# Seven blocks of 128 query columns for the maxima, and new orders on TensorE

## The chip, the core and the metric

The kernel runs on one core of a Trainium2 chip. The time is the device time of one execution in microseconds. Three runs of the kernel before took 1652.04 to 1652.82 us, median 1652.7.

## The reference, cut to what matters

A cross-attention layer and a routed feed-forward layer, both with a residual. Only the attention is touched.

```python
# x: (16, 224, 512); context: (16, 750, 384); 16 heads of 32
q = layernorm(x) @ Wq.T + bq
k = context @ Wk.T + bk
v = context @ Wv.T + bv
attn = softmax(einsum('bihd,bjhd->bhij', q, k) / sqrt(32))
x = x + einsum('bhij,bjhd->bihd', attn, v) @ Wo.T + bo
```

The softmax of each query and head runs over 750 keys.

## The kernel before, in words

The attention is cut into 64 groups: 16 batches of four groups, each with four heads (NG = 4, GH = 4). Python unrolls the loop over g, and each engine runs its own written list of steps, `first`, `second`, `third` or `fourth` by the group's position in its batch (g % 4). Semaphores alone tie the engines together. The expert layer follows after the last group.

While TensorE works on the scores of group g, it also prepares group g + 1 (maxima) and g + 2 (projections). Its steps are these; the short names are used in the tables below.

- Q: `project_q(g + 2)`, 12 matmuls of 224 columns. K0, K1: `project_k(g + 2, 0 or 1)`, 9 matmuls each.
- X0 to X7: `score_for_max(g + 1, u)` (L1529). A block of query columns of one head (QP = 112 of the 224) is the stationary operand, the keys in two halves of 376 columns are the moving one. The queries lie in `q_own`, a copy for each head with the other heads' rows set to zero. There is one pair of PSUM banks, X, so each block waits until DVE has taken the maximum of the block before (`max_done`).
- mT: `transpose_max(g + 1)` turns the column maxima round. ACT negates them into `mneg` (`max_out`, L765), behind the group's last exponential in its list, and SP sends them by DMA (`put_max`, L391) into a row of `qst`, so that the score matmuls subtract the maximum. Score 0 of the next group waits for that DMA.
- S0 to S11: `score(g, s)`, two matmuls of 224 columns into one of two PSUM banks S; ACT takes the exponential (`exps`, L773), so S(s) waits for the exponential s - 2.
- W0, W1, W2: `values(g, p)`, fp32 matmuls of the exponentials with V, after exponentials 4p to 4p + 3; W2 of a group runs in the next group's list.
- den: `denominators(g - 1)`, fp32 matmuls over `psum_p`, the sum of the exponentials that POOL builds in five additions of two tiles (`add_step`).
- In single positions: V4a to V5b and V0a to V3b, `project_v` in two parts; Oa, Ob and Oc, Od, `project_o` for the two halves of the rows; xT0, xT1, yT0, yT1, transposes; lg0, lg1, `logits`.

DVE's list is the same in all positions up to small additions: maximum 0, q_lo, maximum 1, maximum 2, k_lo 0, maximum 3, k_lo 1, (in the second position two `xT_rest`), invert and normalise of the denominators, maximum 4, `o_lo` (L1089), maxima 5, 6, 7, with `residual`, `keep_logits`, `y_stats` or `ln_stats` beside or behind the last ones. `o_lo` computes the low part of the output from `o_s` and `oT_h`, both in SBUF.

The blocks Q, K, V, O, den, transposes, logits and mT share three PSUM banks M in the fixed order of `misc_units` (L90): each takes the bank that was used three units earlier, and waits until it is freed. In the second position den takes the bank of K1, which DVE's k_lo 1 (L1057) frees.

In the first position POOL adds the output bias to `x_res` (`add_bo`, L498) at the end of its list, when SP's load of `x_res` (L358) has landed; that load waits for the stores of `x_res` (L368), which SP issues behind the copies of q and k into `qst` and `kst`. POOL's additions 3 and 4 of the group follow in the next position's list.

Of the kernel before, what the change touches and what calls it, by code (L numbers as in the profile page):

```python
# [6 lines left out]
F32R = mybir.dt.float32r  # L7
# [4 lines left out]
P = 128  # L12
# [8 lines left out]
GH = 4  # L21
# [46 lines left out]
XU = 8  # L68
# [50 lines left out]
def expert_phase(nc, x1_d, w1, b1, w2, b2, centroids, w_route, ident_d, gates_dram, out):  # L119
    x, ctxT, wqT, bq, wkT, bk, wvT, bv, woT, bo, ident, x1 = SCRATCH["attention"]  # L120
    with ExitStack() as es:
# [50 lines left out]
        mneg = sb("mneg", [XU, QP], F32R)  # L172
# [159 lines left out]
        with nc.Block() as block:  # L332
# [352 lines left out]
            def _(act):  # L685
# [335 lines left out]
            def _(dve):  # L1021
# [44 lines left out]
                def maximum(g, u):  # L1066
# [5 lines left out]
                    dve.tensor_reduce(mx[0:QP, u:u + 1], X[0:QP, :, 0:HALF[0][1]], AX.XY, ALU.max).then_inc(max_done, 1)  # L1072
# [99 lines left out]
                def first(g, b):  # L1172
# [13 lines left out]
                    maximum(g + 1, 7)  # L1186
# [3 lines left out]
                def second(g, b):  # L1190
# [16 lines left out]
                    maximum(g + 1, 7)  # L1207
                    residual(b - 1, 1)

                def third(g, b):  # L1210
# [13 lines left out]
                    maximum(g + 1, 7)  # L1224
                    y_stats(b - 1)

                def fourth(g, b):
# [13 lines left out]
                    maximum(g + 1, 7)  # L1241
# [197 lines left out]
            def _(pe):  # L1439
# [89 lines left out]
                def score_for_max(g, u):  # L1529
                    if not 0 <= g < GROUPS:  # L1530
                        return
                    j, qt = u // QT, u % QT
                    if u == 0:
                        pe.wait_ge(kh_done, 2 * (g + 1))
                    if qt == 0:
                        pe.wait_ge(own_done, GH * g + j + 1)
                    if g or u:
                        pe.wait_ge(max_done, XU * g + u)
                    for i, (off, w) in enumerate(HALF):
                        last = pe.matmul(X[0:QP, i, 0:w], q_own[:, g % 2, j, QP * qt:QP * (qt + 1)],  # L1540
                                         kh_s[:, g % 2, off:off + w], start=True, stop=True)
                    last.then_inc(x_full, 1)

                def transpose_max(g):
# [4 lines left out]
                    pe.transpose(out[0:XU, 0:QP], mx[0:QP, :], id_s[0:QP, 0:QP]).then_inc(full, 1)  # L1549
# [79 lines left out]
                def first(g, b):  # L1629
# [4 lines left out]
                    values(g - 1, 2)  # L1634
                    score(g, 0)
                    score(g, 1)
                    score_for_max(g + 1, 2)
                    project_k(g + 2, 1)
                    score_for_max(g + 1, 3)
                    score(g, 2)  # L1640
                    denominators(g - 1)
                    project_v(b, 4, 0)
                    score_for_max(g + 1, 4)
                    score(g, 3)
                    score(g, 4)
                    project_v(b, 4, 1)
                    project_v(b, 5, 0)
                    score(g, 5)
                    project_v(b, 5, 1)
                    score_for_max(g + 1, 5)  # L1650
                    score(g, 6)
                    score(g, 7)
                    values(g, 0)
                    score(g, 8)
                    score_for_max(g + 1, 6)
                    values(g, 1)
                    score(g, 9)
                    score_for_max(g + 1, 7)
                    logits(b - 2, 0)
                    logits(b - 2, 1)  # L1660
                    score(g, 10)
                    score(g, 11)
                    transpose_max(g + 1)

                def second(g, b):
                    score_for_max(g + 1, 0)
                    project_q(g + 2)
                    score_for_max(g + 1, 1)
                    project_k(g + 2, 0)
                    values(g - 1, 2)  # L1670
                    score(g, 0)
                    score_for_max(g + 1, 2)
                    score(g, 1)
                    score(g, 2)
                    project_k(g + 2, 1)
                    score_for_max(g + 1, 3)
                    score(g, 3)
                    score(g, 4)
                    transpose_x(b + 1, 0)
                    transpose_x(b + 1, 1)  # L1680
                    values(g, 0)
                    denominators(g - 1)
                    score(g, 5)
                    project_o(b - 1, 0, 0)
                    score_for_max(g + 1, 4)
                    project_o(b - 1, 0, 1)
                    score(g, 6)
                    score(g, 7)
                    score_for_max(g + 1, 5)
                    score(g, 8)  # L1690
                    values(g, 1)
                    score_for_max(g + 1, 6)
                    project_o(b - 1, 1, 0)
                    score(g, 9)
                    score_for_max(g + 1, 7)
                    project_o(b - 1, 1, 1)
                    score(g, 10)
                    score(g, 11)
                    transpose_max(g + 1)

                def third(g, b):
                    project_q(g + 2)
                    score_for_max(g + 1, 0)
                    project_k(g + 2, 0)
                    score_for_max(g + 1, 1)
# [5 lines left out]
                    score(g, 2)  # L1711
                    score_for_max(g + 1, 3)
                    project_v(b + 1, 0, 0)
                    project_v(b + 1, 0, 1)
# [179 lines left out]
```

## Time and profile before

| what | value |
|---|---|
| median of three runs | 1652.7 us |
| profiled execution, its time | 1648.43 us |
| its span | 1646.6 us |
| TensorE busy | 1524.2 us, 93% |
| DVE busy | 1030.6 us, 63% |
| ACT busy | 944.2 us, 57% |
| POOL busy | 1080.2 us, 66% |
| maxima on DVE (L1072) | 512, 480.6 us busy |
| matmuls of score_for_max (L1540) | 1024, 272.0 us busy |

Busy times are of the whole span, with the expert layer, whose work starts some 1330 us in. Matmuls overlap their neighbours in these records, so a share of busy time is not a share of peak.

### The profile page before, as it was taken

How to read it: one execution, taken by the hardware profiler on the slowest of the kernel's cores; microseconds unless marked ns; L12 is line 12 of the kernel's file. 1: busy time of each engine (PE TensorE's matmuls, PEld its weight loads, DVE VectorE, ACT ScalarE, POOL GpSimd, SP SyncE). 2: the span in 40 equal slices, each digit the busy share in tenths (PEclk: the TensorE clock that was granted, in tenths of full speed). 3: DMA queues.
4: the chain of work that ended last, by engine and by line, in shares of the span. 5: the costliest groups of instructions: out<-in, count | busy, mean ns of one | idle time of the engine just before them, and what ended most of it. 6: DMA issues, size and time to landing. Idle time of an engine off the chain costs nothing.

```text
span 1646.6 us, 33344 instructions
## 1 busy us (share of the span) xinstructions
PE 1524.2 (93%) x11534; PEld 1247.4 (76%) x11534; DVE 1030.6 (63%) x1475; ACT 944.2 (57%) x2055; POOL 1080.2 (66%) x931
## 2 busy tenths in 40 slices
PE   4899999999999999999999999999999743899997
PEld 4777777778787878787877877877777433798996
DVE  5556666666666676766666666666665568344443
ACT  4456666666666666666666666665665440455554
POOL 3366767676767677776676777777775740477675
PEclk9999999999999999999999999999999765899999
DMA  7556666666667676767666757676756733578785
GB/s 193 97 81 111 101 134 123 110 124 108 127 110 134 111 129 112 131 110 139 112 130 107 136 101 144 101 140 101 140 91 120 187 122 35 136 135 147 135 148 90
DMA packets 113394, 199.29 MB, mean 121 GB/s; under 512 B 20448, under 2 KB 49280, under 8 KB 113104
## 3 DMA queue, kind: packets, MB, share of 16 engines
q1 hardware_dynamic: 98992, 165.81, 54.4%
q0 software_dynamic: 14240, 31.35, 10.5%
q8 instruction: 98, 1.61, 0.5%
q14 instruction: 64, 0.52, 0.1%
HBM read 64.29 MB, written 38.66 MB: 63 GB/s over the span
## 4 chain that ended last, share of the span: by engine, by line
PE 86%; DVE 5%; ACT 3%; POOL 2%; issue 1%; DMA 1%; POOLq 0%; DVEq 0%; SPq 0%; ACTq 0%
PE M L320 12%; PE S L1563 12%; PE M L321 12%; PE M L322 12%; PE X L1540 11%; PE O L1579 10%; ACT pr L781 2%; PE M L1825 2%; PE X L1807 2%; PE X L1808 2%; PE X L1806 2%; PE M L1826 2%; PE M L1827 2%; PE M L1590 2%; PE S L1796 2%
## 5 line engine op out<-in xcount | busy, mean ns | idle before, releaser
L1072 DVE TENSOR_REDUCE mx<-X 112x1 f32<-112x752 f32 x512 | 480.6, 939 | 356.0 <-PE X L1540 353.9
L491 POOL TENSOR_TENSOR psum_p<-psum_p,pr 125x896 f32<-125x896 f32 x256 | 543.9, 2124 | 172.6 <-ACT pr L781 149.1
L781 ACT ACTIVATE pr<-S 125x448 f32<-125x448 f32 x768 | 395.0, 544 | 224.4 <-PE S L1563 216.6
L1563 PEld LDWEIGHTS S<-qst,kst 128*125 128x125 f32 x1536 | 234.7, 189 | 113.0 <-ACT pr L781 51.2
L1563 PE MATMUL S<-qst,kst 128*125 128x224 f32 x1536 | 287.3, 291 | 27.1 <-ACT pr L781 21.2
L1540 PE MATMUL X<-kh_s,q_own 128*112 128x376 f32 x1024 | 272.0, 347 | 8.4 <-DVE mx L1072 7.9
L1540 PEld LDWEIGHTS X<-kh_s,q_own 128*112 128x112 f32 x1024 | 153.9, 176 | 48.0 <-issue 26.8
L1579 PE MATMUL O<-pr,v 125*32 125x224 f32 x3072 | 188.6, 364 | 1.7 <-ACT pr L781 1.7
L488 POOL TENSOR_TENSOR psum_p<-pr 125x896 f32<-125x896 f32 x64 | 135.6, 2119 | 80.1 <-ACT pr L781 79.9
L475 POOL TENSOR_TENSOR ctx_l<-ctx_r,ctx_h 128x750 fp32r<-128x750 f32 x48 | 85.4, 1811 | 74.7 <-ACT ctx_h L696 74.7
L320 PE MATMUL M<-ctx_h,wk_h 128*128 128x376 f32 (+1 forms) x384 | 130.0, 339 | 0.0
L321 PE MATMUL M<-ctx_l,wk_h 128*128 128x376 f32 (+1 forms) x384 | 129.4, 337 | 0.0
L322 PE MATMUL M<-ctx_h,wk_l 128*128 128x376 f32 (+1 forms) x384 | 128.8, 335 | 0.0
L1579 PEld LDWEIGHTS O<-pr,v 125*32 125x32 f32 x3072 | 81.3, 110 | 62.3 <-issue 23.1
L662 POOL DMA_INDIRECT out<-y_out,table_t x63 | 99.9, 1586 | 41.4 <-ACT y_out L1003 23.3
L654 POOL DMA_INDIRECT xg<-rows_d,table_x x63 | 62.4, 990 | 86.3 <-DVE settled L1400 43.0
L320 PE MATMUL M<-wv_h,ctx_h 128*125 128x512 f32 x288 | 116.8, 405 | 0.0
L322 PE MATMUL M<-wv_h,ctx_l 128*125 128x512 f32 x288 | 113.6, 394 | 0.0
L321 PE MATMUL M<-wv_l,ctx_h 128*125 128x512 f32 x288 | 113.5, 394 | 0.0
L1079 DVE RECIPROCAL M<-M 128x224 f32<-128x224 f32 x64 | 99.8, 1559 | 21.7 <-PE M L1590 21.6
L738 ACT ACTIVATE q_own<-qh_s,own 128x224 fp32r<-128x224 f32 x256 | 102.6, 472 | 2.1
L1062 DVE SCALAR_TENSOR_TENSOR kl_s<-M,bk_s,kh_s 128x376 fp32r<-128x376 f32 (+1 forms) x128 | 77.0, 602 | 14.3 <-ACT kh_s L749 14.1
(222 smaller groups left out, 3005.1 us busy)
## 6 DMA issues: line engine op xcount, KB each, us to landing
kst<-kh_s SPq DMA_DIRECT2D x128, 375.0 KB, 7.3
kst<-kl_s SPq DMA_DIRECT2D x64, 375.0 KB, 10.4
ctx_r<-ctxT SPq DMA_DIRECT2D x48, 375.0 KB, 12.2
qst<-qh_s SPq DMA_DIRECT2D x128, 112.0 KB, 2.8
rows_d<-x_res SPq DMA_DIRECT2D x32, 448.0 KB, 10.6
w_l<-w SPq DMA_DIRECT2D x16, 512.0 KB, 7.0
x_ln<-x SPq DMA_DIRECT2D x17, 448.0 KB, 11.0
qst<-ql_s SPq DMA_DIRECT2D x64, 112.0 KB, 3.0
```

The lines of the kernel that those rows point to most:

```text
L320: pe.matmul(out, lhs[0], rhs[0], start=first, stop=False)
L321: pe.matmul(out, lhs[0], rhs[1], start=False, stop=False)
L322: return pe.matmul(out, lhs[1], rhs[0], start=False, stop=last)
L488: pool.tensor_tensor(out=total, in0=tiles[0], in1=tiles[1], op=ALU.add).then_inc(sum_step, 1)
L491: pool.tensor_tensor(out=total, in0=total, in1=tiles[half], op=ALU.add).then_inc(sum_step, 1)
L662: pool.indirect_dma_start(out=out[:, :], out_offset=bass.IndirectOffsetOnAxis(ap=table_t[:, i:i + 1], axis=0), in_=y_out[:, i % YO, :], in ...
L738: act.activation(q_own[:, g % 2, j, :], qh_s[:, g % 2, :], ACT.Copy, scale=own[:, j:j + 1]).then_inc(own_done, 1)
L781: act.activation(pr[0:KP, (3 * g + p) % 2, j, :, :], S[0:KP, n % SB, 0:2 * NQ].rearrange("p (i n) -> p i n", i=2), ACT.Exp).then_inc(exp_d ...
L1072: dve.tensor_reduce(mx[0:QP, u:u + 1], X[0:QP, :, 0:HALF[0][1]], AX.XY, ALU.max).then_inc(max_done, 1)
L1540: last = pe.matmul(X[0:QP, i, 0:w], q_own[:, g % 2, j, QP * qt:QP * (qt + 1)], kh_s[:, g % 2, off:off + w], start=True, stop=True)
L1563: last = pe.matmul(S[0:KP, n % SB, NQ * h:NQ * (h + 1)], kst[:, i, j, o:o + KP], qst[:, i, j, :], start=True, stop=True)
L1579: last = pe.matmul(O[HD * j:HD * (j + 1), 0:NQ], v[0:KP, 2 * p + i, HD * j:HD * (j + 1)], pr[0:KP, (3 * g + p) % 2, j, i, :], start=(p == ...
```

## The change

The 4 x 224 = 896 query columns of the four heads are taken as one row of columns and cut into seven blocks of 128 in place of eight of 112. XU becomes 7, a block waits for the last head that it reaches into, and the maximum and the transpose use all 128 partitions. `mneg` becomes 7 x 128. DVE's lists lose maximum 7. TensorE's four lists are written anew. The lists of ACT and of POOL, and SP's, stay as they are.

```diff
-XU = 8
+XU = GH * NQ // P
...
-        mneg = sb("mneg", [XU, QP], F32R)
+        mneg = sb("mneg", [XU, P], F32R)
...
-                    act.activation(mneg[:, :], bank_of("mT", g)[0:XU, 0:QP], ACT.Copy, scale=-1.0).then_inc(freed("mT", g), 1)
+                    act.activation(mneg[:, :], bank_of("mT", g)[0:XU, 0:P], ACT.Copy, scale=-1.0).then_inc(freed("mT", g), 1)
...
-                    dve.tensor_reduce(mx[0:QP, u:u + 1], X[0:QP, :, 0:HALF[0][1]], AX.XY, ALU.max).then_inc(max_done, 1)
+                    dve.tensor_reduce(mx[:, u:u + 1], X[:, :, 0:HALF[0][1]], AX.XY, ALU.max).then_inc(max_done, 1)
...
                     maximum(g + 1, 6)
-                    maximum(g + 1, 7)
...
-                    j, qt = u // QT, u % QT
+                    own_q = q_own[:, g % 2, :, :].rearrange("p j n -> p (j n)")
                     if u == 0:
                         pe.wait_ge(kh_done, 2 * (g + 1))
-                    if qt == 0:
-                        pe.wait_ge(own_done, GH * g + j + 1)
+                    pe.wait_ge(own_done, GH * g + (P * (u + 1) - 1) // NQ + 1)
                     if g or u:
                         pe.wait_ge(max_done, XU * g + u)
                     for i, (off, w) in enumerate(HALF):
-                        last = pe.matmul(X[0:QP, i, 0:w], q_own[:, g % 2, j, QP * qt:QP * (qt + 1)],
+                        last = pe.matmul(X[:, i, 0:w], own_q[:, P * u:P * (u + 1)],
                                          kh_s[:, g % 2, off:off + w], start=True, stop=True)
...
-                    pe.transpose(out[0:XU, 0:QP], mx[0:QP, :], id_s[0:QP, 0:QP]).then_inc(full, 1)
+                    pe.transpose(out[0:XU, 0:P], mx[:, :], id_s[:, :]).then_inc(full, 1)
```

TensorE's lists in the short names, before and after:

```
first   before  X0 Q K0 X1 W2 S0 S1 X2 K1 X3 S2 den V4a X4 S3 S4 V4b V5a S5 V5b X5 S6 S7 W0 S8 X6 W1 S9 X7 lg0 lg1 S10 S11 mT
        after   X0 Q K0 X1 S0 W2 S1 X2 K1 S2 den X3 S3 V4a V4b S4 X4 S5 V5a V5b S6 X5 S7 lg0 W0 lg1 S8 X6 S9 W1 S10 mT S11
second  before  X0 Q X1 K0 W2 S0 X2 S1 S2 K1 X3 S3 S4 xT0 xT1 W0 den S5 Oa X4 Ob S6 S7 X5 S8 W1 X6 Oc S9 X7 Od S10 S11 mT
        after   X0 Q X1 W2 K0 S0 S1 X2 S2 K1 X3 S3 xT0 xT1 den X4 S4 S5 Oa Ob S6 S7 W0 X5 Oc S8 W1 S9 S10 X6 Od S11 mT
third   before  Q X0 K0 X1 S0 W2 S1 X2 K1 S2 X3 V0a V0b S3 den X4 V1a S4 S5 V1b X5 W0 S6 X6 S7 S8 S9 X7 W1 S10 mT S11
        after   Q W2 X0 K0 X1 K1 S0 X2 S1 V0a X3 S2 V0b S3 S4 den W0 S5 X4 V1a V1b S6 X5 S7 S8 X6 S9 W1 S10 S11 mT
fourth  before  X0 Q W2 X1 K0 X2 S0 S1 K1 S2 X3 den V2a S3 V2b X4 S4 S5 V3a V3b X5 S6 S7 W0 X6 W1 S8 S9 yT0 yT1 X7 S10 mT S11
        after   X0 Q K0 X1 W2 S0 S1 X2 K1 S2 X3 den S3 V2a V2b V3a S4 S5 V3b S6 S7 W0 X4 W1 X5 yT0 yT1 S8 X6 S9 S10 mT S11
```

## Rows read from the trace of the kernel before

**Rows 1.** Windows, 400 to 600 us: busy us and count of each engine, clock, DMA
```profile
400.00:600.00 200.00, 197.02 (x1537) 158.49 (x1534) 133.81 (x188) 123.31 (x278) 142.53 (x128) 1.00 0.66 116
```

**Rows 2.** Timeline of TensorE, one batch: start, duration, instruction, idle before
```profile
607.47 0.26 PE L1549 MATMUL M<-id_s,mx 112*8 112x112 f32 x1
...
684.95 0.58 PE L1540 MATMUL X<-kh_s,q_own 128*112 128x376 f32 x2
686.36 0.47 PE L1563 MATMUL S<-qst,kst 128*125 128x224 f32 x2 [0.83 <-ACT pr L781]
686.67 0.26 PE L1549 MATMUL M<-id_s,mx 112*8 112x112 f32 x1
```

**Rows 3.** Timeline of TensorE in a fourth position: starts of neighbouring blocks
```profile
671.68 0.51 PE L1540 MATMUL X<-kh_s,q_own 128*112 128x376 f32 x2
672.02 0.60 PE L1563 MATMUL S<-qst,kst 128*125 128x224 f32 x4
...
674.22 0.50 PE L1540 MATMUL X<-kh_s,q_own 128*112 128x376 f32 x2
674.65 0.58 PE L1590 MATMUL M<-psum_p,ones 125*32 125x224 f32 x8
```

**Rows 4.** The page's groups: busy us, mean ns, idle before; weight loads of score_for_max
```profile
L1540 PEld LDWEIGHTS X<-kh_s,q_own 128*112 128x112 f32 x1024 | 153.9, 176 | 48.0 <-issue 26.8
```

**Rows 5.** Waits of TensorE: us in total, times, longest
```profile
PE S L1563 <- ACT pr L781: 21.2, 36, 2.3
...
PE X L1540 <- DVE mx L1072: 7.9, 10, 1.7
```

**Rows 6.** Groups by line and shape: K's weight loads, POOL's bias additions
```profile
L320 PEld LDWEIGHTS M<-ctx_h,wk_h 128*128 128x128 f32 x384 | 73.7, 192 | 0.0
...
L507 POOL TENSOR_TENSOR x_res<-x_res,bo_s 112x512 f32<-112x512 f32 x30 | 38.1, 1290 | 28.2 <-DMA x_res<-x 28.2
```

**Rows 7.** Timeline of DVE, tail of a fourth position
```profile
678.99 2.33 DVE L1093 SCALAR_TENSOR_TENSOR oT_l<-o_s,bv_s,oT_h 128x224 fp32r<-128x224 f32 x1
...
682.93 0.94 DVE L1072 TENSOR_REDUCE mx<-X 112x1 f32<-112x752 f32 x1 [0.75 <-PE X L1540]
```

**Rows 8.** Timeline of SyncE's queue, end of a fourth position
```profile
608.81 0.71 SPq L393 DMA_DIRECT2D qst<-mneg  x1
```

**Rows 9.** Chain of waits, near the last group
```profile
1282.88 1.79 DMA qst<-mneg
```

**Rows 10.** Timeline of all engines, a second position (it begins at 627.4)
```profile
629.80 2.54 POOL L507 TENSOR_TENSOR x_res<-x_res,bo_s 112x512 f32<-112x512 f32 x2 [2.33 <-DMA x_res<-x]
...
632.30 4.38 POOL L491 TENSOR_TENSOR psum_p<-psum_p,pr 125x896 f32<-125x896 f32 x2
...
635.12 0.51 PE L1540 MATMUL X<-kh_s,q_own 128*112 128x376 f32 x2
...
636.52 0.60 DVE L1062 SCALAR_TENSOR_TENSOR kl_s<-M,bk_s,kh_s 128x374 fp32r<-128x374 f32 x1
...
637.55 0.56 PE L1590 MATMUL M<-psum_p,ones 125*32 125x224 f32 x8
...
641.17 0.44 DVE L1093 SCALAR_TENSOR_TENSOR oT_l<-o_s,bv_s,oT_h 128x224 fp32r<-128x224 f32 x1
```

**Rows 11.** Timeline of ACT, a fourth position: V3 copied out, exponentials 6 and 7
```profile
680.66 0.39 ACT L761 ACTIVATE v<-M 125x256 f32<-125x256 f32 x1 [0.98 <-PE M L322]
...
681.23 0.98 ACT L781 ACTIVATE pr<-S 125x448 f32<-125x448 f32 x2
```

**Rows 12.** Timeline of POOL, the same position: its additions
```profile
678.96 2.12 POOL L488 TENSOR_TENSOR psum_p<-pr 125x896 f32<-125x896 f32 x1
682.28 4.34 POOL L491 TENSOR_TENSOR psum_p<-psum_p,pr 125x896 f32<-125x896 f32 x2 [1.20 <-ACT pr L781]
```

**Rows 13.** Timeline of DVE after the last maxima: subtractions of the expert weights
```profile
1301.28 1.23 DVE L1149 TENSOR_TENSOR w_l<-w_l,w_h 128x1024 fp32r<-128x1024 f32 x1 [0.91 <-ACT w_h L846]
1303.57 4.99 DVE L1149 TENSOR_TENSOR w_l<-w_l,w_h 128x1024 fp32r<-128x1024 f32 x2 [1.07 <-ACT w_h L846]
```

More of the change, by code:

```diff
@@ L1633, in first @@
                     score_for_max(g + 1, 1)
[L1634 to L1705, printed above, removed]
                     score(g, 0)
@@ L1733, in third, with second @@
                     score(g, 11)
+                def second(g, b):
+                    score_for_max(g + 1, 0)
+                    project_q(g + 2)
+                    score_for_max(g + 1, 1)
+                    values(g - 1, 2)
+                    project_k(g + 2, 0)
+                    score(g, 0)
+                    score(g, 1)
+                    score_for_max(g + 1, 2)
+                    score(g, 2)
+                    project_k(g + 2, 1)
+                    score_for_max(g + 1, 3)
+                    score(g, 3)
+                    transpose_x(b + 1, 0)
+                    transpose_x(b + 1, 1)
+                    denominators(g - 1)
+                    score_for_max(g + 1, 4)
+                    score(g, 4)
+                    score(g, 5)
+                    project_o(b - 1, 0, 0)
+                    project_o(b - 1, 0, 1)
+                    score(g, 6)
+                    score(g, 7)
+                    values(g, 0)
+                    score_for_max(g + 1, 5)
+                    project_o(b - 1, 1, 0)
+                    score(g, 8)
+                    values(g, 1)
+                    score(g, 9)
+                    score(g, 10)
+                    score_for_max(g + 1, 6)
+                    project_o(b - 1, 1, 1)
+                    score(g, 11)
+                    transpose_max(g + 1)
@@ new lines, in third @@
+                def third(g, b):
+                    project_q(g + 2)
+                    values(g - 1, 2)
+                    score_for_max(g + 1, 0)
+                    project_k(g + 2, 0)
+                    score_for_max(g + 1, 1)
+                    project_k(g + 2, 1)
+                    score(g, 0)
+                    score_for_max(g + 1, 2)
+                    score(g, 1)
+                    project_v(b + 1, 0, 0)
+                    score_for_max(g + 1, 3)
+                    score(g, 2)
+                    project_v(b + 1, 0, 1)
+                    score(g, 3)
+                    score(g, 4)
+                    denominators(g - 1)
+                    values(g, 0)
+                    score(g, 5)
+                    score_for_max(g + 1, 4)
+                    project_v(b + 1, 1, 0)
+                    project_v(b + 1, 1, 1)
+                    score(g, 6)
+                    score_for_max(g + 1, 5)
+                    score(g, 7)
+                    score(g, 8)
+                    score_for_max(g + 1, 6)
+                    score(g, 9)
+                    values(g, 1)
+                    score(g, 10)
+                    score(g, 11)
+                    transpose_max(g + 1)
```

45 lines of the change are left out of this document (21 added, 24 removed).

## The prediction, made before the changed kernel ran

> **What bounds the kernel now.** I read the mean work of each engine in a steady stretch first, then the page's groups for the touched line, then who waited for whom on TensorE, and last the timelines of each engine over one batch of four groups. In the stretch TensorE is busy 197.02 of 200 us with the clock granted in full, DVE 133.81, ACT 123.31, POOL 142.53 [rows 1]. TensorE is what a group's length follows; the other three set only where it stalls. A group is about 20 us, a batch 686.67 - 607.47 = 79.20 us [rows 2].
>
> A pipelined matmul's busy time overlaps its neighbour's, so I price blocks by start to next start. One score_for_max takes 672.02 - 671.68 = 0.34 us [rows 3], though its two matmuls show 0.51 busy there. In front of a block of values or denominators (fp32 operands) the same block takes 674.65 - 674.22 = 0.43 [rows 3]: TensorE pays 0.09 for the change of operand kind. It is paid on entering values and denominators and on leaving any fp32 block, transposes and logits among them.
>
> Over that batch the blocks and changes leave 2.75 us of real waits: none in the first position, 0.77 in the second, 0.76 in the third, 1.2 in the fourth. The idle column shows only part of a wait, since a modelled tail covers the start of it: the largest, 684.95 + 0.34 to 686.36, is 1.07 us, of which the row shows 0.83 [rows 2]. The others are read in the same way, each as the time by which a block outlasts its price. All waits for exponentials show 21.2 us of idle time, all waits of a score_for_max for the maxima 7.9 [rows 5].
>
> **What the change does, term by term.** The summary speaks of four engines; the diff reorders only TensorE. ACT and POOL keep their lists, DVE loses the eighth maximum. So new places on TensorE meet old places elsewhere.
>
> (a) One score_for_max less in each group: 4 x 0.34 = -1.38 us a batch. The blocks that stay stream the same two times 376 columns. Their stationary operand widens from 112 to 128 columns: its load goes from 176 ns [rows 4] to the 192 ns that K's loads take [rows 6]. I take nothing for it, because X and K blocks keep the same 0.17 us per 376 columns with either width; with the loads exposed it would be 16 ns x 14 x 4 = +0.9 a batch. On DVE a maximum still reads 752 elements of each partition: 0.94 us [rows 7], one fewer, hidden. The copy out becomes 7x128 instead of 8x112 and its DMA carries the same 3.5 KB: nothing. Transposing needs one wait fewer.
> The Trainium skill speaks against this point: TensorE: Matmul & The Clock Gate, Part 2, says that the time of a weight load grows with its columns. The loads of rows 4 and 6 agree (176 to 192 ns); the page also says that the next load runs beside the current matmul, and by that the sum stays, while by the first sentence alone the +0.9 would be due.
>
> (b) Changes of operand kind, counted by the rule above: 10, 7, 9 and 10 in the four positions before, 8, 9, 7 and 10 after (values now stand between the logits in the first; denominators adjoin values in the third but no longer in the second). Two fewer: 2 x 0.09 = -0.19.
>
> (c) The waits. I lay each new list out by the block times and look at each semaphore.
>
> First position: maxima come at least 1.65 us apart (0.60 from the start of the block to DVE, 0.94, about 0.1 back); everything fits, also score 0, which moves ahead of values(g - 1, 2) by 1.0 us and needs the negated maxima. Their DMA is issued 608.81 - 607.47 = 1.34 after the transpose [rows 2, 8] and took 1.79 where the chain of waits ran through it [rows 9]: 3.1, against 3.9 in the new list. If it needed a microsecond more, that would cost 0.2 a batch. Waits 0, as before.
>
> Second: denominators moves ahead of values(g, 0) and so 1.3 us nearer to two things. It takes the PSUM bank of K1, which DVE frees after maximum 3 and k_lo: 2.0 us after that score_for_max starts (635.12 to 637.12) [rows 10]. In the new list only a score and two transposes (1.4 with the block itself) lie between: a wait of 0.6. And it needs POOL's last sum, which ended 636.68 before (two additions of 2.19 behind two bias additions that waited 2.33 for the x_res load) [rows 10], 9.3 us into a group that began 627.4; that wait is 28.2 / 14 = 2.0 on average [rows 6], so POOL ends 9.0 in. The load is issued by SP behind a store that starts in the first position, so a first position shorter by 0.4 puts it 0.4 later: 9.4. TensorE comes 8.8 in. Together 0.75 (bounds: 0.6, the bank alone, and 1.4, should the load be 0.8 late). Score 2 waits 0.17 for the first exponential. Sum 0.92.
>
> Third: score_for_max 3 now comes 1.25 us after number 2: waits 0.39. project_v(b + 1, 1) ends right before score 6; ACT copies its two halves first and reaches exponential 6 0.57 us after it starts on them (680.66, 681.23) [rows 11], and one exponential is 0.54: score 8 waits 0.58. score_for_max 6 waits 0.23. Sum 1.20.
>
> Fourth: its tail is the worst place. In the kernel before, maximum 4 is long done when o_lo runs. o_lo is the one steady operation of DVE with both inputs in SBUF; it starts 678.99 and takes 2.33 us, ending 0.24 after POOL's addition of 678.96 to 681.08 [rows 7, 12]; in the other three positions it takes 0.44 [rows 10]. Now score_for_max 4 stands behind values(g, 0), so maximum 4 ends 1.2 us after exponential 7, when POOL is in its second addition (it began 682.28, 0.07 after exponential 7 ended [rows 11, 12]). o_lo stands behind maximum 4 and in front of 5. It gets through when the addition ends, 2.45 after exponential 7; maximum 5 ends 3.35, score_for_max 6 starts 3.4, its maximum ends 4.95, the transpose starts 5.05. Before, it started 686.67 - 682.21 = 4.46 [rows 2, 11]. Exponential 7 itself comes 0.3 earlier. In waits: 0.2 for score_for_max 5, 0.7 for 6, 0.9 at the transpose: 1.80. The old wait of 1.07 on exponential 8 goes, but what is late next is the maximum of block 6. If o_lo were not held, the transpose would come 0.75 sooner.
>
> New waits 0 + 0.92 + 1.20 + 1.80 = 3.92, old 2.75: +1.17.
>
> **The sum.** -1.38 - 0.19 + 1.17 = -0.40 us a batch. The full pattern runs for 62 groups, 15.5 batches: -6.2 us. At the start, where three maxima in a row set the pace, one is saved in a place where there are still three: -0.35, inside the rounding. After the last group nothing changes. The profiled execution took 1648.43 us (span 1646.6): 1642.2. The runs shown have their median 4.3 above the profiled one: 1652.7 - 6.2 = 1646.5 us.
>
> **Rivals.**
> 1. The waits stay as they were, and all of 1.38 + 0.19 comes through: 15.5 x 1.57 = 24 us, 1628. For it: TensorE is busy nearly throughout, and idle shown is small [rows 1, 5]; it needs the order to dodge the banks and the second addition, which the rows above speak against. A nearer form, in which only o_lo in the fourth position isn't held, gives -0.40 - 0.75 = -1.15 a batch, -18, 1635. Chance of the two together 0.22.
> 2. Slower: o_lo is passed over by POOL. Its second and third additions follow each other (4.34 us for two [rows 12]). If the third got in before o_lo, o_lo would end 4.6 after exponential 7, and all behind it 2.2 later: 15.5 x 2.2 = +34 on the forecast, 1680. Against it: where both engines press, DVE's two-input subtractions and POOL's additions alternate: two in 4.99 us after one alone in 1.23 [rows 13]. It need not be the whole addition: from 0.4 us a batch the gain is gone, from 0.6 the kernel is slower by what can be told, and if it happens in two batches of five it is 0.9 on average, 1660, which I take as this rival's value. Chance 0.17.
> The Trainium skill, SBUF — State Buffer, Terms, calls the pair of ports that DVE and GpSimd share exclusive, held for the full instruction. By it o_lo waits for one addition as rows 7 and 12 show; it doesn't say who is next, which is what this rival turns on.
> 3. No change: denominators in the second position waits 1.1 in place of 0.75, as it does when the x_res load lands 0.5 later than on average: -0.05 a batch, 1652. Chance 0.18.
> 4. The change does not do what it says, since three engines keep their order: true of the text of it, and already in the sum.
>
> **How the numbers follow.** Forecast 0.43 (1640 to 1649), rivals as above. What a measurement here can tell from no change is 0.2%, 3.3 us. Faster by more: the forecast's 0.43 less a little at its upper edge, and rival 1: 0.61. Within: 0.2. Slower: 0.19. The range for 8 in 10 reaches down over rival 1's nearer half and most of its farther, 1629, and up over rival 3 and the first part of 2, to 1656.
>
> **What the changed profile would show.** 896 matmuls of score_for_max at 0.17 us start to start, so the width is free. TensorE's waits for the maxima up from 7.9 to over 15 us, at the transpose above all in the fourth position; waits of denominators for POOL or DVE in the second position in most batches, where there were none; o_lo still 2 us or so once a batch, but now between maxima 4 and 5 and shorter (it meets an addition already running). A batch of 78.8 us. I am wrong if a batch is under 78.2 or above 79.2: then one of the three lists of waits is wrong, and the position whose length differs says which.

## The result, and the profile after

The changed kernel took 1659.15 us (median of 5 runs, 1657.51 to 1660.19), the one before 1652.04 (1651.11 to 1652.82). The ratio is 1.0043, interval 1.0028 to 1.0057: slower by 7.1 us, where 6.2 us faster was forecast. The profiled execution took 1657.51 us, its span is 1655.6.

The page after, the groups that answer to [rows 4, 5] (busy us, mean ns, idle before):

```profile
PE 1505.5 (91%) x11406; PEld 1234.8 (75%) x11406; DVE 950.7 (57%) x1411; ACT 944.1 (57%) x2055; POOL 1079.9 (65%) x931
...
L1072 DVE TENSOR_REDUCE mx<-X 128x1 f32<-128x752 f32 x448 | 420.2, 938 | 461.4 <-PE X L1535 461.1
...
L1535 PE MATMUL X<-kh_s,q_own 128*128 128x376 f32 x896 | 246.7, 357 | 21.6 <-DVE mx L1072 21.1
L1535 PEld LDWEIGHTS X<-kh_s,q_own 128*128 128x128 f32 x896 | 139.3, 191 | 69.3 <-issue 67.2
```

The work that was to go is gone: 448 maxima in place of 512, 896 matmuls in place of 1024, TensorE's busy time down by 18.7 us. The span is 9 us longer. In windows over the stretch of [rows 1] (columns as there), TensorE is busy 3.7 us less at the same full clock, and DVE 15.4 less:

```profile
400.00:600.00 200.00, 193.33 (x1522) 155.79 (x1521) 118.42 (x175) 123.39 (x277) 141.18 (x127) 1.00 0.65 115
```

The waits of TensorE (us in total, times, longest) say what fills it. Those of score_for_max for a maximum went from 7.9 us [rows 5] to 21.1, and those of the transpose from 3.0 to 12.1. Denominators waits for `kl_s`, which it did not before, and for POOL 12.0 us in 5 times where it was 7.7 in 2 (the long one, of the last group, stands in both):

```profile
PE X L1535 <- DVE mx L1072: 21.1, 53, 1.2
PE S L1558 <- ACT pr L781: 16.0, 35, 2.3
...
PE M L1544 <- DVE mx L1072: 12.1, 17, 1.1
PE M L1585 <- POOL psum_p L491: 12.0, 5, 7.5
...
PE M L1585 <- DVE kl_s L1062: 7.4, 13, 0.7
```

The batch that answers to [rows 2] is 687.46 - 607.93 = 79.53 us long, and at its end 0.69 us idle show at the transpose, for the last maximum:

```profile
607.93 0.27 PE L1544 MATMUL M<-id_s,mx 128*7 128x128 f32 x1 [0.69 <-DVE mx L1072]
...
683.74 0.58 PE L1535 MATMUL X<-kh_s,q_own 128*128 128x376 f32 x2 [0.23 <-DVE mx L1072]
684.16 0.93 PE L1463 MATMUL M<-id_s,x_res 112*128 112x112 f32 x8
...
685.75 0.58 PE L1535 MATMUL X<-kh_s,q_own 128*128 128x376 f32 x2 [0.44 <-DVE mx L1072]
686.17 0.60 PE L1558 MATMUL S<-qst,kst 128*125 128x224 f32 x4
687.46 0.27 PE L1544 MATMUL M<-id_s,mx 128*7 128x128 f32 x1 [0.69 <-DVE mx L1072]
...
687.78 0.51 PE L1535 MATMUL X<-kh_s,q_own 128*128 128x376 f32 x2
```

A block of score_for_max that had to wait for a maximum also takes longer itself: 684.16 - 683.74 = 0.42 us to the next block, and 0.42 again at 685.75, where others take 0.35. In the means below, its second matmul starts 0.25 us after its first, where in a block that found its maximum done it starts 0.18 after.

For everything below I took the start of the first block behind each group's last score and transpose from TensorE's timeline, and averaged the distances over groups 12 to 55 by position. A block's price is the same kind of mean, start to next start. These are lengths in us:

```
kernel                         first  second third  fourth  batch
before                         19.51  20.69  18.97  20.08   79.26
before, another chip           19.52  20.82  18.98  20.06   79.37
changed                        19.26  21.06  18.95  20.41   79.68
changed, another chip          19.29  21.05  18.94  20.41   79.69
e1 old lists less X7           19.21  20.76  19.01  20.08   79.06
e2 eight blocks, 128 wide      19.64  20.79  19.15  20.10   79.69
e3 old second                  19.28  20.49  18.96  20.41   79.13
e4 old fourth                  19.24  21.11  18.95  20.15   79.46
e6 den later                   19.26  21.26  18.95  20.41   79.89
e7 o_lo first                  19.26  21.02  18.94  20.11   79.33
e8 old second and o_lo first   19.27  20.37  18.94  20.11   78.69
e10 old first                  19.21  22.81  18.95  20.41   81.38
e11 old third                  19.25  21.10  18.73  20.33   79.42
e12 e8, exponential 6 first    19.28  20.48  18.95  20.11   78.82
```

A batch repeats within 0.1 us from one chip to another, a position within 0.03, but for the unchanged second position (0.13). A saving of 1.38 us a batch was due; the first position gained 0.25, the third 0.02, the second lost 0.37 and the fourth 0.33: +0.42 together, over the 15 batches from group 4 to 63 +6.3 us. Before group 4 the changed kernel was 2.6 us ahead (130.3 us against 132.9), so it ends group 63 3.8 us late. In the second pair of profiles (e5 and e9, below) it was only 0.5 ahead there (132.2 against 132.7), so the 2.6 is not a firm gain. The rest lies in the expert layer, which the change doesn't touch: there the two profiles differ by 5 us. The expert loop took 228.2 us in the first profile of before and 231.7 in a second one, 232.9 in that of after. This difference goes with the chip, or with what else differed between the measurements on it, and not with the kernel. From the start of the first matmul of the first tile to that of the last one, the four profiles e1 to e4, of one chip, show 230.4 to 231.9 us, the eight of e5 to e12, of two other chips, 235.6 to 237.4; the first profile of before, with 232.2, is like the former, that of after, with 236.9, like the latter. At most 1 or 2 us of it can be put down to the change.

### The profile page after: what moved, and what is told of

Read it like the earlier page. It is cut to its first block, busy times and chain, and to the rows that moved or that the text cites. A ratio compares the mean times of both kernels' runs of the same rounds, so it can differ in the third digit from the quotient of the medians.

```text
span 1655.6 us, 33216 instructions
## 1 busy us (share of the span) xinstructions
PE 1505.5 (91%) x11406; PEld 1234.8 (75%) x11406; DVE 950.7 (57%) x1411; ACT 944.1 (57%) x2055; POOL 1079.9 (65%) x931
## 4 chain that ended last, share of the span: by engine, by line
PE 80%; DVE 11%; POOL 3%; ACT 2%; issue 2%; DMA 1%; POOLq 0%; SPq 0%; ACTq 0%; DVEq 0%
PE M L320 11%; PE M L321 11%; PE M L322 11%; PE X L1535 10%; PE S L1558 10%; PE O L1574 9%; DVE mx L1072 5%; POOL psum_p L491 2%; PE M L1585 2%; PE X L1799 2%; PE X L1797 2%; PE X L1798 2%; PE M L1816 2%; PE M L1817 2%; PE M L1818 2%
## 5 line engine op out<-in xcount | busy, mean ns | idle before, releaser
L1072 DVE TENSOR_REDUCE mx<-X 128x1 f32<-128x752 f32 x448 | 420.2, 938 | 461.4 <-PE X L1535 461.1
L1558 PEld LDWEIGHTS S<-qst,kst 128*125 128x125 f32 x1536 | 244.0, 189 | 84.1 <-ACT pr L781 49.6
L1535 PE MATMUL X<-kh_s,q_own 128*128 128x376 f32 x896 | 246.7, 357 | 21.6 <-DVE mx L1072 21.1
L1535 PEld LDWEIGHTS X<-kh_s,q_own 128*128 128x128 f32 x896 | 139.3, 191 | 69.3 <-issue 67.2
L1416 DVE TENSOR_TENSOR y_raw<-M,b_all 128x512 f32<-128x512 f32 x63 | 43.6, 692 | 69.5 <-PE M L1818 65.7
```

The costliest lines, as they stand in the source:

```text
L1072: dve.tensor_reduce(mx[:, u:u + 1], X[:, :, 0:HALF[0][1]], AX.XY, ALU.max).then_inc(max_done, 1)
L1535: last = pe.matmul(X[:, i, 0:w], own_q[:, P * u:P * (u + 1)], kh_s[:, g % 2, off:off + w], start=True, stop=True)
L1558: last = pe.matmul(S[0:KP, n % SB, NQ * h:NQ * (h + 1)], kst[:, i, j, o:o + KP], qst[:, i, j, :], start=True, stop=True)
```

## The experiments

Each ran beside the unchanged kernel on one chip. Its median there was 1646.8 for e1 to e4, 1652.1 for e5 to e8 and 1651.7 for e9 to e12, so kernels are compared by ratio.

**e1: the seven blocks alone.** TensorE keeps its old lists.

```diff
 (all of the change but TensorE's lists, and in each of the four old lists)
-                    score_for_max(g + 1, 7)
```

> Seven blocks of 128 as in the changed kernel, but TensorE runs the four lists of the kernel before, with score_for_max 7 struck out. Theory A (the blocks save work, the new lists give it back in waits): the first, second and third position each lose one block of 0.35 us; in the fourth the block stood in a wait for exponential 8 and its going frees nothing. 3 x 0.35 x 15.5 = 16 us below the kernel before, 1636, a batch of 78.2 us. Theory B (128 columns or 128 partitions cost what the eighth block saved): within 3 us of the kernel before or above it, whatever the list.

Measured 1638.23 us, ratio 0.9943 (0.9931 to 0.9956): 8.5 us faster. So seven blocks do pay, and the new lists cost more than they bring: 1.0043 against 0.9943, some 16 us. But only half of the expected gain came. The batch is 0.20 us shorter, not 1.1: the first position kept 0.30 of its saved block, the other three kept nothing. Waits of e1 on TensorE:

```profile
PE S L1558 <- ACT pr L781: 27.3, 40, 2.3
PE M L1585 <- POOL psum_p L491: 15.1, 22, 7.5
...
PE X L1535 <- DVE mx L1072: 6.2, 7, 1.7
```

With one block fewer ahead of them, exponentials are late (21.2 us before, 27.3 now) and denominators meets POOL's last sum 22 times. The larger part of what the profile shows is at the start: group 4 begins at 126.9 us against 132.9. That is not shown to be the seven blocks. The clock column (the one before the last two) of the stretch from 15 to 133 us, before and then e1, differs:

```profile
15.00:133.00 118.00, 101.91 (x672) 83.51 (x673) 68.31 (x89) 61.70 (x133) 48.98 (x32) 0.94 0.58 105
15.00:133.00 118.00, 103.60 (x712) 85.59 (x713) 67.53 (x92) 65.11 (x143) 53.69 (x36) 0.97 0.59 108
```

TensorE's granted clock stood at the lower of its two levels (1.2 GHz) for 13.7 us there in the kernel before and for 6.8 in e1; by an estimate from these two numbers that alone is up to 3.4 us. The one maximum that goes before group 0, where maxima follow each other without a break, is worth 1.6 (14.1 us from the first block to group 0 against 15.7). e4, with three of the four new lists, starts group 4 at 127.0, the changed kernel at 130.3 and 132.2, so the start moves with more than the blocks.

**e2: the width alone.** The kernel before, with its eight blocks and old lists, but each block takes 128 columns: it reaches 16 columns into the next one, whose maxima it doesn't use. The last one starts 16 columns early, so its queries subtract the maxima of their neighbours.

```diff
-                        last = pe.matmul(X[0:QP, i, 0:w], q_own[:, g % 2, j, QP * qt:QP * (qt + 1)],
+                        last = pe.matmul(X[:, i, 0:w], flat_q[:, min(QP * u, XU * QP - P):min(QP * u, XU * QP - P) + P],
```

> The kernel before with its eight blocks and old lists, but each block's stationary operand is 128 columns wide in place of 112 and the maximum is taken over 128 partitions; the extra 16 maxima are not used, and the last block starts 16 columns early, so its queries subtract their neighbours' maxima. Theory A: in the changed kernel a block of score_for_max that is followed by a block of the same kind starts 0.353 us ahead of it, before 0.345: 8 ns x 32 blocks = 0.25 us a batch, 4 us in all, 1656. Theory B (width is what made the change slower): a batch longer by 1.5 us or more, 1675. If width is free: 1652.

Measured 1656.0, ratio 1.0059 (1.0044 to 1.0074): 9.2 us slower with the same count of matmuls. The weight loads went from 176 ns [rows 4] to 191, by the page of e2:

```profile
L1539 PEld LDWEIGHTS X<-kh_s,q_own 128*128 128x128 f32 x1024 | 166.2, 191 | 47.3 <-issue 39.3
```

The batch is 0.43 longer, on average 13 ns for each of 32 blocks (0.32 and 10 ns against the second profile of before). The width is not free. But the rise is uneven: half of the blocks grew by 7 ns or less, and four by 36 to 63. One of the four is X1 of the second position, which starts 0.15 us after maximum 0 ends, as blocks do that wait for their maximum: it went from 0.370 to 0.424 us. So part of the 0.43 is the loop of block, maximum and next block, which got tight, and not the wider operand by itself. The number of result rows changes with the width too; what in a block takes the time isn't told apart.

**e3 and e4: one old list.** The changed kernel with the old second list, and with the old fourth.

```diff
 second
- X0 Q X1 W2 K0 S0 S1 X2 S2 K1 X3 S3 xT0 xT1 den X4 S4 S5 Oa Ob S6 S7 W0 X5 Oc S8 W1 S9 S10 X6 Od S11 mT
+ X0 Q X1 K0 W2 S0 X2 S1 S2 K1 X3 S3 S4 xT0 xT1 W0 den S5 Oa X4 Ob S6 S7 X5 S8 W1 X6 Oc S9 Od S10 S11 mT
 fourth, in the other kernel
- X0 Q K0 X1 W2 S0 S1 X2 K1 S2 X3 den S3 V2a V2b V3a S4 S5 V3b S6 S7 W0 X4 W1 X5 yT0 yT1 S8 X6 S9 S10 mT S11
+ X0 Q W2 X1 K0 X2 S0 S1 K1 S2 X3 den V2a S3 V2b X4 S4 S5 V3a V3b X5 S6 S7 W0 X6 W1 S8 S9 yT0 yT1 S10 mT S11
```

> The changed kernel with TensorE's second list as in the kernel before, less block 7; the other three new. Theory A: the wait of denominators for K1's bank (0.6 in the changed kernel) and one change of operand kind go, the second position falls from 21.0 to 20.4 us: -0.6 x 15.5 = -9 us against the changed kernel, 1650. Rival: that wait is only moved, the denominators then wait for POOL or the next position pays: 1657 to 1660.

> The changed kernel with TensorE's fourth list as in the kernel before, less block 7. Theory A: score_for_max 4 stands before V3 again, o_lo runs during POOL's first addition and holds nothing up; what is late is exponential 8 and with it score 10. Fourth position from 20.4 to 20.1 us: -0.3 x 15.5 = -5 us, 1654. Rival (the waits for maxima in that tail cost nothing, since exponential 8 comes as late): unchanged, 1659.

e3: 1641.26, ratio 0.9966 (0.9953 to 0.9979). Against the changed kernel's 1.0042 (e5, below) that is 12.6 us less; the second position went from 21.06 to 20.49. e4: 1646.32, ratio 0.9994 (0.9980 to 1.0008), about 8 us less; the fourth went from 20.41 to 20.15. Both new lists are worse than the old, the second by more. The batches account for some 8.5 us in e3 and 3.4 in e4. Of the rest of e4 some 3 us lie before group 4 (127.0 against 130.3) and are not the fourth list's for certain.

**e5 and e9** are the changed and the unchanged kernel once more. e5 gave 1658.95, ratio 1.0042 (1.0026 to 1.0058), and the long expert layer came again.

> The changed kernel once more, beside the others of this call. Two things are asked. Its time against the kernel before on this chip: 1.0043 if the first measurement holds. And its expert layer: in its first profile the tiles took 237.3 us from the first matmul of the first tile to the last, 5 more than in the kernel before, with 3.1 us of idle marked issue in front of the bias matmul. If that belongs to the kernel it comes again (237); if it is of one execution, 232.

> The kernel before, unchanged, for a profile taken beside the others. Its profile so far shows the expert layer's tiles at 228.2 us from first to last matmul, with one stall at issue of over 0.2 us after the first tile; the profiles of the changed kernel show 233, with seven or so. If those stalls belong to the chip or the execution and not to the change, this profile shows them or not as the others of this call do, and the attention alone carries the difference: a batch of 79.26 against 79.68.

e9 gave 1651.32 against 1651.68, ratio 0.9997: this is the noise. Its span of 1650.1 is 3.5 us longer than in the first profile of before, with the last score of group 63 within 0.4 us of it. So those microseconds come and go in the expert layer of one and the same kernel, and go with the chip, as said above. What makes them is open.

**e6: denominators behind score 5** in the second position, so that it need not wait for its bank.

```diff
-                    denominators(g - 1)
                     score_for_max(g + 1, 4)
                     score(g, 4)
                     score(g, 5)
+                    denominators(g - 1)
                     project_o(b - 1, 0, 0)
```

> The changed kernel; in the second position denominators stands behind score_for_max 4 and scores 4 and 5, 0.8 us later. Theory A: its wait for K1's bank (0.77 us in the changed kernel) is filled with that work, one more change of operand kind costs 0.09, nothing behind it moves: second position from 21.06 to 20.4 us, -0.65 x 15.5 = -10 us against the changed kernel. Rival (the wait only moves, since the reciprocal and with it exponential 4 come as late and score 6 waits): 21.0, no gain.

1662.47, ratio 1.0064 (1.0046 to 1.0082): no gain, rather a loss of 3.5. The wait of denominators for `kl_s` is gone from the waits (it showed 7.4 us in 13 times), and the second position still grew by 0.20. In the timeline of e6 the block of denominators runs without a wait, and three others get the idle time: block X4, which now meets maximum 3, and scores 6 and 7 behind Ob, 0.37, 0.28 and 0.41 us over the price:

```profile
637.07 0.51 PE L1535 MATMUL X<-kh_s,q_own 128*128 128x376 f32 x2
...
638.70 0.59 PE L1535 MATMUL X<-kh_s,q_own 128*128 128x376 f32 x2
639.12 0.59 PE L1558 MATMUL S<-qst,kst 128*125 128x224 f32 x4
639.65 0.59 PE L1585 MATMUL M<-psum_p,ones 125*32 125x224 f32 x8
...
643.30 0.91 PE L1558 MATMUL S<-qst,kst 128*125 128x224 f32 x4
```

X4 starts 1.63 us after X3, about the least that was seen with a maximum in between. The two scores cover 0.84 us where they should cover 0.43. A wait was moved, not taken away.

**e7: `o_lo` ahead of maximum 4** in DVE's fourth list, the rest as changed.

```diff
                     normalise(g - 1)
-                    maximum(g + 1, 4)
                     o_lo(g - 1)
+                    maximum(g + 1, 4)
                     maximum(g + 1, 5)
```

> The changed kernel; in DVE's fourth list o_lo stands in front of maximum 4, nothing else is moved. Theory A: o_lo then meets POOL's first addition, where DVE has nothing else to do; maximum 5 starts when its block is full, score_for_max 6 about 0.4 earlier, the transpose 0.6: fourth position from 20.41 to 19.85 us, -0.55 x 15.5 = -8.5 us against the changed kernel. Rival (exponential 8, behind the copies of the transposes, sets score 10 and so the end): -0.1 a batch, -2 us.

1651.90, ratio 1.0001 (0.9992 to 1.0010), 7 us less than the changed kernel; the fourth position went from 20.41 to 20.11. DVE's tail of the changed kernel, then that of e7:

```profile
682.65 0.94 DVE L1072 TENSOR_REDUCE mx<-X 128x1 f32<-128x752 f32 x1 [4.08 <-PE X L1535]
683.51 1.24 DVE L1093 SCALAR_TENSOR_TENSOR oT_l<-o_s,bv_s,oT_h 128x224 fp32r<-128x224 f32 x1
684.67 0.93 DVE L1072 TENSOR_REDUCE mx<-X 128x1 f32<-128x752 f32 x1
686.37 0.94 DVE L1072 TENSOR_REDUCE mx<-X 128x1 f32<-128x752 f32 x1 [0.76 <-PE X L1535]
```

```profile
677.62 2.32 DVE L1093 SCALAR_TENSOR_TENSOR oT_l<-o_s,bv_s,oT_h 128x224 fp32r<-128x224 f32 x1 [0.74 <-ACT oT_h L799]
680.96 0.94 DVE L1072 TENSOR_REDUCE mx<-X 128x1 f32<-128x752 f32 x1 [1.02 <-PE X L1535]
682.66 0.94 DVE L1072 TENSOR_REDUCE mx<-X 128x1 f32<-128x752 f32 x1 [0.76 <-PE X L1535]
684.38 0.94 DVE L1072 TENSOR_REDUCE mx<-X 128x1 f32<-128x752 f32 x1 [0.77 <-PE X L1535]
```

In e7 `o_lo` takes 2.32 us and costs nothing, since DVE has 4 us free there; in the changed kernel its shorter 1.24 stand between two maxima of the chain that ends the group. Of the 0.75 that its hold was worth by the forecast 0.30 came, although `o_lo` is gone from the chain altogether. What is left is the chain itself. TensorE's side of the same place in e7:

```profile
683.75 0.59 PE L1535 MATMUL X<-kh_s,q_own 128*128 128x376 f32 x2
...
685.46 0.27 PE L1544 MATMUL M<-id_s,mx 128*7 128x128 f32 x1 [0.40 <-DVE mx L1072]
```

The last maximum ends at 684.38 + 0.94 = 685.32 and the transpose starts 0.14 later. Its block began 0.15 after the maximum before it (683.60), and so did the one before. On average the steps from X4 to X5 to X6 to the transpose are 1.74, 1.71 and 1.71 us in e7, and 1.74, 2.00 and 1.71 in the changed kernel. The new fourth list puts three such steps in a row behind W0, and only the 0.29 of `o_lo` could be taken out of them.

**e8: the new first, third and fourth lists, the old second, and `o_lo` first.** Both edits above in one kernel.

> Seven blocks; first, third and fourth lists of the changed kernel, the second list of the kernel before less block 7, and o_lo in front of maximum 4 in DVE's fourth list. If the savings of e3_old_second (a batch of 79.13) and e7 add up: 79.13 - 0.55 = 78.6 us a batch, 0.65 below the kernel before, 10 us from the batches and some 3 at the start: 0.992 of the kernel before. If POOL's chain into the next third position takes it back, as the other kernels hint (denominators waits for POOL there once the second position is short): 0.996.

1639.43, ratio 0.9926 (0.9913 to 0.9939), 12.7 us below the kernel before and 19 below the changed one. A batch is 78.69. It is the lowest of all that ran, though its interval overlaps those of e1 and e12. Its waits on TensorE:

```profile
PE S L1558 <- ACT pr L781: 16.5, 39, 2.3
...
PE X L1535 <- DVE mx L1072: 14.8, 39, 1.2
...
PE M L1585 <- POOL psum_p L491: 10.2, 3, 7.5
PE M L1544 <- DVE mx L1072: 7.5, 16, 1.1
```

**e10: the old first list** in the changed kernel.

```diff
 first
- X0 Q K0 X1 S0 W2 S1 X2 K1 S2 den X3 S3 V4a V4b S4 X4 S5 V5a V5b S6 X5 S7 lg0 W0 lg1 S8 X6 S9 W1 S10 mT S11
+ X0 Q K0 X1 W2 S0 S1 X2 K1 X3 S2 den V4a X4 S3 S4 V4b V5a S5 V5b X5 S6 S7 W0 S8 X6 W1 S9 lg0 lg1 S10 S11 mT
```

> The changed kernel with TensorE's first list as in the kernel before, less block 7. In e1_seven_old, with all lists old, the first position took 19.21 us, in the changed kernel 19.26: the new first list neither costs nor gains. Expected within 0.1 us a batch, 2 us in all, of the changed kernel. Rival (each list only fits its neighbours, and the old first in front of the new second costs at the seam): +0.3 a batch, +5 us.

1671.14, ratio 1.0115 (1.0100 to 1.0129), 12 us slower than the changed kernel, though its own position is 0.05 shorter. In its profile the second position grew by 1.75. That execution took 1681.45 us, 10 more than the median of the five: 1.70 us a batch would be 26 us, and the median shows 12, so the usual growth is nearer to half of what the profile shows. Waits of denominators for POOL there, by the waits of e10, went to 31.1 us:

```profile
PE M L1585 <- POOL psum_p L491: 31.1, 16, 7.5
```

One second position each, first the changed kernel, then e10 (timelines of SyncE's queue, TensorE and POOL):

```profile
626.20 0.32 SPq L358 DMA_DIRECT2D x_res<-x  x1
627.13 0.27 PE L1544 MATMUL M<-id_s,mx 128*7 128x128 f32 x1
629.96 2.54 POOL L507 TENSOR_TENSOR x_res<-x_res,bo_s 112x512 f32<-112x512 f32 x2 [2.10 <-DMA x_res<-x]
632.46 4.37 POOL L491 TENSOR_TENSOR psum_p<-psum_p,pr 125x896 f32<-125x896 f32 x2
637.23 0.59 PE L1585 MATMUL M<-psum_p,ones 125*32 125x224 f32 x8 [0.57 <-DVE kl_s L1062]
```

```profile
634.91 0.32 SPq L358 DMA_DIRECT2D x_res<-x  x1
635.60 0.27 PE L1544 MATMUL M<-id_s,mx 128*7 128x128 f32 x1
639.28 2.53 POOL L507 TENSOR_TENSOR x_res<-x_res,bo_s 112x512 f32<-112x512 f32 x2 [3.25 <-DMA x_res<-x]
641.76 4.37 POOL L491 TENSOR_TENSOR psum_p<-psum_p,pr 125x896 f32<-125x896 f32 x2
646.28 0.58 PE L1585 MATMUL M<-psum_p,ones 125*32 125x224 f32 x8 [1.34 <-POOL psum_p L491]
```

Counted from the transpose, `x_res` is there after 2.83 us in one and 3.68 in the other. POOL's sum ends after 9.70 and 10.53, and denominators starts after 10.10 and 10.68. The old second list reaches denominators later and can hide a part of such a delay, not all of it: in e1, with the old first list too, POOL's sum ends 10.36 us into the position on average and denominators waits for it in 10 of 11 batches; in e8, with the new first list, the sum ends at 9.47 and denominators starts at 10.18. Why the load takes 4.37 us from its issue to POOL's start with the old first list and 3.76 with the new is open.

**e11: the old third list** in the changed kernel.

```diff
 third
- Q W2 X0 K0 X1 K1 S0 X2 S1 V0a X3 S2 V0b S3 S4 den W0 S5 X4 V1a V1b S6 X5 S7 S8 X6 S9 W1 S10 S11 mT
+ Q X0 K0 X1 S0 W2 S1 X2 K1 S2 X3 V0a V0b S3 den X4 V1a S4 S5 V1b X5 W0 S6 X6 S7 S8 S9 W1 S10 mT S11
```

> The changed kernel with TensorE's third list as in the kernel before, less block 7. e1_seven_old has 19.01 us in the third position, the changed kernel 18.95, but there the second position was shorter by 0.3 and denominators of the third waited for POOL. Behind the long new second that wait is gone: third position 18.75, -0.2 a batch, -3 us against the changed kernel. Rival (its length is set by the exponentials behind the copies of V1): 18.95, no difference.

1652.61, ratio 1.0008 (0.9999 to 1.0017), about 6 us less than changed: third position 18.95 to 18.73, fourth 20.41 to 20.33. The old list is the better one here too, behind the new second. Behind the old second it was not: 19.01 us in e1, against 18.96 with the new third in e3. I didn't try it beside e8, where denominators in the old lists might meet POOL as in e1.

**e12: exponential 6 ahead of V1's copies** in ACT's third list, on top of e8. This removes the wait of score 8.

```diff
                     exps(g, 5)
-                    v_out(b + 1, 1)
                     exps(g, 6)
+                    v_out(b + 1, 1)
                     exps(g, 7)
```

> e8_mixed, and in ACT's third list exponential 6 stands in front of the copies of V1 instead of behind them. Score 8 waited 0.56 us for that exponential, whose scores were ready 0.2 before V1; the two copies take 0.55. Third position from 18.94 to 18.6 us, -0.35 x 15.5 = -5 us against e8_mixed, 0.989 of the kernel before. Rival: score 9 waits next for exponential 7, which does not come sooner, and half is lost: -0.15 a batch, 0.991 to 0.992.

1639.69, ratio 0.9930 (0.9915 to 0.9944): the same as e8, and the third position is 18.95 in place of 18.94. TensorE in a third position, e8 first, then e12:

```profile
656.26 0.47 PE L1558 MATMUL S<-qst,kst 128*125 128x224 f32 x2 [0.41 <-ACT pr L781]
656.76 0.59 PE L1535 MATMUL X<-kh_s,q_own 128*128 128x376 f32 x2
...
658.92 0.27 PE L1544 MATMUL M<-id_s,mx 128*7 128x128 f32 x1
```

```profile
655.51 0.91 PE L1558 MATMUL S<-qst,kst 128*125 128x224 f32 x4
656.79 0.58 PE L1535 MATMUL X<-kh_s,q_own 128*128 128x376 f32 x2 [0.37 <-DVE mx L1072]
...
658.95 0.27 PE L1544 MATMUL M<-id_s,mx 128*7 128x128 f32 x1
```

The wait for the exponential is gone and the block of X6 doesn't start sooner: 656.79 against 656.76. It waits for maximum 5, which ends 0.14 before it in both kernels. So in e8 two waits stood side by side, and the one that the profile names was not the only one that set the time.

## Why the prediction was wrong, by its own steps

The forecast was -0.40 us a batch, the trace gave +0.42. Most waits stood where they were forecast; what failed is the sum, in which several small terms of one sign were left out or set too low.

**Term (a), the width, is the first step that failed.** "I take nothing for it, because X and K blocks keep the same 0.17 us per 376 columns" took 176 and 192 ns loads for equal because 0.17 hides a difference of some 4 ns in each matmul. In the means of the changed kernel a block that waits for nothing takes 0.353 us to the next block of its kind, before 0.345: 28 blocks by 8 ns are +0.22 a batch. e2 measured 13 ns a block with the loop through the maximum in it, which would be +0.37. Either lies inside the bound of +0.9 that I had worked out and then set aside. Of the two sentences of the Trainium skill (TensorE: Matmul & The Clock Gate, Part 2), the one by which a load's time grows with its columns had the sign right here; the other, by which the next load runs beside the matmul, took most of it away, since two loads grew by 30 ns together and the block by 8.

**Term (b), the changes of operand kind, was too low.** I let values and denominators be entered from another fp32 block for nothing. By the mean blocks of the changed kernel, the second half of the first logits block takes 0.474 us ahead of W0 where it takes 0.393 ahead of logits before, the second logits block behind W0 takes 0.02 more, and denominators 0.580 ahead of W0 where it takes 0.516 ahead of a score. K0 behind W2 takes 1.650 for 1.54, of which the forecast's 0.09 explains all but 0.02. That is 0.19 a batch. So in place of -0.19 the term was about 0.

**Term (c), the waits, was too low in two ways.** The new ones, measured as the price over the block's own, against the forecast: second position 0.77 for denominators (0.75) and 0.35 for exponential 0 (0.17); third 0.38, 0.56 and 0.30 (0.39, 0.58, 0.23); fourth 0.30, 0.67 and 0.86 (0.2, 0.7, 0.9). Sum 4.19 against 3.92. The old ones, read over all batches in the same way, are 2.85, not 2.75: +1.34 in place of +1.17. And a block that starts on a maximum just done is itself 0.07 us longer, as shown above. That happens in five places of the new lists (X1 of the second position, 0.516 ahead of W2 where such a block takes 0.44; X3 and X6 of the third, X5 and X6 of the fourth), 0.36 a batch together. I had no term for it. The same X1 grew in e2 too, where nothing of its kind changed.

Together 0.22 + 0.19 + 0.17 + 0.36 = 0.94, of a miss of 0.82, so these sizes hold to some 0.1. By position the forecast's own terms come to -0.52, -0.01, -0.08 and +0.26; measured were -0.25, +0.37, -0.02 and +0.33. The second position missed by 0.38, the first by 0.27, the others by less than 0.1. This split is arithmetic on means. Shown by runs are that the width costs (e2), what the second, third and fourth lists cost as they stand (e3, e11, e4) and `o_lo` (e7).

**What was right.** `o_lo` got through when POOL's second addition ended: it ended 2.4 us after exponential 7 (forecast 2.45), block 6 started 3.4 after (3.4), the transpose 5.1 after (5.05). Denominators waits for its bank in most batches: on average the bank is free 9.76 us into the position and POOL's sum there at 9.49. The maxima's waits rose past 15 us. The batch of 79.68 is above the 79.2 at which I had called the forecast wrong, and by position the second is furthest off.

**What was wrong beside the sum.** "If o_lo were not held, the transpose would come 0.75 sooner" left out that the three maxima behind W0 are a chain of their own: e7 gave 0.30. Rival 1's nearer form stood on that 0.75. And 4 x 0.34 is 1.36; the 1.38 needs the mean of 0.345.

**The rivals.** Rival 1 (the waits stay) is refuted, and e1 shows that not even the old order keeps its waits when a block goes: in three of four positions the saved 0.34 us went to exponentials and to POOL's sum. Rival 2 (POOL passes `o_lo` over) is refuted by its 1.24 us, the same in every batch. Rival 3 named a later x_res load; e10 shows the mechanism at full size, but in the changed kernel it is not what ends the wait of denominators in most batches: the bank is. Slower came true through none of them, but through terms that were set too low. The step from the profiled 1648.43 to the median is right in kind: the 4 us lie in the expert layer (e9).

## What to carry to other kernels

Where an engine is busy 98% of the time, a block taken out is worth less than its price: each wait that it covered shows, so walk the list and ask at each semaphore what is late next. A term of some ns in each of thousands of instructions is a term of the sum, and is measured by one kernel that changes it alone; between zero and a bound, don't take zero. Test a rewritten order list by list: of four lists written together here three were worse than the old ones in their own position, and the first, no better in its own, kept its neighbour from growing (by 1.75 us in one profile, by less in most executions). A wait that the profile names can have another one beside it: two of the experiments (e6, e12) took a named wait away and gained nothing. Where a step goes from one engine to another and back, count the steps in a row: their number times the round trip is a length that no reordering of the rest can shorten.

## What the runs showed of the hardware that I had not expected

- Sixteen more columns in the stationary operand cost about 8 ns for each block of two 376-column matmuls in a stretch at full clock, where each load took 15 ns more (176 to 191), though the matmuls are pipelined; with waits for the maxima in it the cost was 13 ns a block (e2).
- A matmul block that starts right after the wait for its maximum (0.15 us after the maximum ends) takes 0.42 us where others take 0.35: its second matmul starts 0.25 us after the first in place of 0.18.
- From one block of score_for_max through its maximum on DVE (0.94 us) to the next block takes at least 1.64 us, in the kernel before and in the changed one, and 1.71 where the first of the two had to wait itself.
- A change of operand kind costs something too where values follow logits or denominators directly: 0.08 and 0.06 us more than between two blocks of logits, or ahead of a score.
- The same kernel's expert loop took 228.2 us in one profile and 231.7 in another, on another chip, at the same mean clock of 0.964 over the execution. Some 2 of the 3.5 us are idle time that the profile calls issue. Over all profiles the expert tiles fall in two groups, over 3 us apart, by chip and not by kernel.
